# Part of a split of x moved from VectorE to GpSimd, and its loads, clears and copies reordered, in a graph layer on one Trainium2 core

## What is computed

```python
msg = x[src] + edge_attr                                  # [E, 128]
agg = jax.ops.segment_sum(msg, dst, num_segments=N)       # [N, 128]
h = relu(agg @ W1 + b1) @ W2 + b2                         # 128 -> 256 -> 128
# h is normalized over all of its elements, then per feature, then gelu
out = _layernorm(x + (gelu(h) + x))
```

## Time and profile before

| what | value |
|---|---|
| median of 3 runs (lowest, highest) | 750.42 us (748.91, 751.47) |
| the profiled execution's own time | 750.58 us |
| its span in the profile | 748.7 us |
| mean granted TensorE clock | 0.98 |
| PE, DVE, ACT, POOL busy | 92%, 85%, 57%, 16% of the span |
| DMA, mean over the span | 161 GB/s |

### The profile page before, as it was taken

One profiled execution on the slowest core, in us unless ns is written; L12 is line 12 of the kernel. 1 busy time (PEld: TensorE's weight loads), 2 busy tenths in 40 slices (PEclk: granted clock), 3 DMA queues, 4 the chain that ended last, 5 costly groups with the idle time before them and its releaser, 6 DMA issues.

```text
span 748.7 us, 25387 instructions
## 1 busy us (share of the span) xinstructions
PE 692.2 (92%) x9473; PEld 628.3 (84%) x9473; DVE 633.3 (85%) x1067; ACT 424.8 (57%) x962; POOL 116.9 (16%) x91
## 2 busy tenths in 40 slices
PE   4748999999999999999999999999999999999964
PEld 4736888999889988999889988899889998888843
DVE  6698889899899898998989889899898998835576
ACT  6634466546664476645665466645756456514447
POOL 2132110111011110111101110411101111000024
PEclk9997999999999999999999999999999999999986
DMA  7298665356554564536635466255662566400006
GB/s 166 84 338 275 210 202 175 109 178 220 162 177 143 179 215 135 188 130 214 210 103 191 157 220 210 76 193 182 214 189 82 184 214 199 120 16 0 0 1 171
DMA packets 90297, 120.42 MB, mean 161 GB/s; under 512 B 8824, under 2 KB 88190, under 8 KB 90075
## 3 DMA queue, kind: packets, MB, share of 16 engines
q1 hardware_dynamic: 83588, 113.93, 47.0%
q0 software_dynamic: 5776, 5.39, 2.7%
q10 hardware_dynamic: 912, 0.83, 0.6%
HBM read 116.03 MB, written 4.03 MB: 160 GB/s over the span
## 4 chain that ended last, share of the span: by engine, by line
PE 78%; ACT 7%; DMA 5%; DVE 4%; issue 3%; POOL 2%; ACTq 0%; SPq 0%; DVEq 0%; POOLq 0%
PE bank L845 40%; PE bank L787 18%; PE bank L738 10%; ACT counts L617 6%; PE bank L893 3%; PE bank L883 3%; PE bank L752 3%; DMA edges<-in_edge_attr_dram 1%; DMA agg<-pool_m 1%; POOL pool_m L545 1%; PE bank L767 1%; DMA listed<-agg 1%; DMA near<-listed,row_slot 1%; DVE pool_m L1137 1%; DMA begins<-listed,tile_slot 0%
## 5 line engine op out<-in xcount | busy, mean ns | idle before, releaser
L617 ACT CAST counts<-bank 128x490 fp32r<-128x490 f32 x600 | 320.2, 605 | 234.5 <-PE bank L787 231.6
L845 PE MATMUL bank<-counts,x_hi 128*128 128x250 f32 x1225 | 309.0, 292 | 8.9 <-ACT counts L617 8.9
L845 PE MATMUL bank<-counts,x_lo 128*128 128x250 f32 x1225 | 293.5, 279 | 0.0
L845 PEld LDWEIGHTS bank<-counts,x_hi 128*128 128x128 f32 x1225 | 231.0, 189 | 15.2 <-ACT counts L617 14.4
L1137 DVE TENSOR_TENSOR pool_m<-value_row,turned_lo 128x3328 bf16<-128x3328 bf16 (+1 forms) x125 | 229.2, 1834 | 12.8 <-PE bank L787 11.1
L845 PEld LDWEIGHTS bank<-counts,x_lo 128*128 128x128 f32 x1225 | 232.4, 190 | 0.0
L787 PE MATMUL bank<-pool_m 128*128 128x98 bf16 x3125 | 195.3, 210 | 8.2 <-DVE pool_m L1137 4.0
L787 PEld LDWEIGHTS bank<-pool_m 128*128 128x128 bf16 x3125 | 158.4, 99 | 28.1 <-ACT counts L617 7.0
L1137 DVE TENSOR_TENSOR pool_m<-value_row,turned_key 128x2548 bf16<-128x2548 bf16 (+1 forms) x125 | 179.7, 1437 | 0.0
L505 POOL DMA_INDIRECT near<-listed,row_slot x27 | 52.4, 1940 | 495.4 <-DVE tile_slot L992 465.3
L738 PE MATMUL bank<-edges,onehot 128*32 128x128 f32 x3228 | 122.1, 285 | 8.0 <-DMA edges<-in_edge_attr_dram 4.1
(11 more groups left out here) (157 smaller groups left out, 467.0 us busy)
## 6 DMA issues: line engine op xcount, KB each, us to landing
edges<-in_edge_attr_dram SPq DMA_DIRECT2D x134, 768.0 KB, 5.1
out_dram<-pool_m SPq DMA_DIRECT2D x12, 256.0 KB
x_in<-in_x_dram SPq DMA_DIRECT2D x4, 448.0 KB, 5.3
agg<-in_dst_dram SPq DMA_DIRECT2D x1, 768.0 KB
agg<-in_src_dram ACTq DMA_DIRECT2D x1, 768.0 KB
listed<-agg SPq DMA_DIRECT2D x1, 768.0 KB
begins<-listed,tile_slot POOLq DMA_INDIRECT x28, 4.0
near<-listed,row_slot POOLq DMA_INDIRECT x27
```

The costliest lines, as they stand in the source:

```text
L617: nc.scalar.copy(counts[:, :, at:at + NODES], cps[k % RING][:, 0:NODES * NT].rearrange("p (n q) -> p q n", q=NT)).then_inc(banks_free, 1)
L845: last = nc.tensor.matmul(sps[:, 0:CHUNK], part[:, q, :], counts[:, q, at:at + CHUNK], start=(q == 0 and part is x_hi), stop=(q == NT - 1 ...
```

## The change

The change does this:

- `EARLY` is 2, not 4: two pieces of x are loaded ahead of the list, and the remaining 34 tiles (not 20) after the first `gather_near`.
- SP loads H0 as soon as the first `gather_begins` has landed, ahead of the rest of x.
- GpSimd clears columns from 3072 on right behind `gather_begins(0)`; ScalarE clears columns 0 to 3071 by a copy of a zero once the destinations are turned. VectorE waits for both.
- ScalarE makes `x_hi` of pieces 0 and 1 between its two searches, and of the other five when the rest of x is there.
- VectorE makes `x_lo` of pieces 0 and 1 ahead of `stage_row(0)`; GpSimd makes the other five behind `gather_near(1)`, with `gather_begins(2)` after three of them.
- The widening of chunk 1's words moves from VectorE to ScalarE, behind the copies of the first two groups' sums.

```diff
-EARLY = 4
+EARLY = 2
@@ SBUF
+        zero = mv
@@ sync, behind the stores of the list (load and load_pair moved up unchanged)
+            sp.wait_ge(begins_loaded, 16)
+            load(0, 0, 0, 1)
             sp.wait_ge(near_loaded, 16)
...
-            for i in range(2 * LEAD):
+            for i in range(1, 2 * LEAD):
                 load(i // 2, i % 2, i % HALVES, i + 1)
@@ gpsimd
             gather_begins(0)
+            pool.memset(agg[:, GROUP:], 0.0).then_inc(agg_zeroed, 1)
             gather_near(0)
             gather_begins(1)
-            pool.wait_ge(turned, TURNS)
-            pool.memset(agg[:, :], 0.0).then_inc(agg_zeroed, 1)
-            with pool.Fori(1, CHUNKS + 2) as c:
+            gather_near(1)
+            for i in range(EARLY, NT // PIECE):
+                if i == 5:
+                    gather_begins(2)
+                pool.wait_ge(x_high, i + 1)
+                at = slice(i * PIECE, (i + 1) * PIECE)
+                pool.tensor_tensor(x_lo[:, at, :], x_in[:, at, :], x_hi[:, at, :].bitcast(F32), ALU.subtract
+                                   ).then_inc(x_split, 1)
+            with pool.Fori(2, CHUNKS + 2) as c:
                 gather_near(c)
                 gather_begins(c + 1)
@@ scalar
-            search(1)
-            search(2)
...
+            search(1)
             act.wait_ge(x_loaded, 16 * EARLY)
             split_high(0, EARLY)
+            search(2)
+            act.wait_ge(turned, TURNS)
+            nc.scalar.copy(agg[:, 0:GROUP], zero[:, 0:1].to_broadcast([P, GROUP])).then_inc(agg_zeroed, 1)
...
             for g in range(LEAD):
+                if g == GPC:
+                    widen_words(1)
                 copy_sums(g, g % GPC)
@@ vector
             dve.memset(no_edges[:, :], NO_EDGE)
+            dve.memset(zero[:, :], 0.0)
...
+            for i in range(EARLY):
+                split_x(i)
             stage_row(0)
...
             stage_row(1)
-            for i in range(NT // PIECE):
-                split_x(i)
             split_words(1)
-            widen_words(1)
             join_keys(1)
             stage_tile(2)
-            dve.wait_ge(agg_zeroed, 1)
+            dve.wait_ge(agg_zeroed, 2)
```

More of the change, by code:

```diff
@@ L399, in _ @@
             sp.dma_start(listed_full[0:EVEN, :], src_rows[0:EVEN, :]).then_inc(listed_stored, 16)
-            sp.wait_ge(near_loaded, 16)
-            for a, b in ((0, EVEN_LAST), (EVEN_LAST, LAST)):
-                sp.dma_start(x_in[a:b, NT - 1, :], x[(NT - 1) * P + a:(NT - 1) * P + b, :]).then_inc(x_rest_loaded, 16)
-            sp.dma_start(x_in[:, EARLY * PIECE:NT - 1, :], x[EARLY * PIECE * P:(NT - 1) * P, :].rearrange("(t p) d -> p t d", p=P)
-                         ).then_inc(x_rest_loaded, 16)
             def load(g, k, u, free):
@@ L414, in load_pair @@
                          p * (2 * PER_PAIR) + (2 * LEAD + FREED_BY[i] + 1 + HALVES))
-            for i in range(2 * LEAD):
+            sp.wait_ge(begins_loaded, 16)
+            load(0, 0, 0, 1)
+            sp.wait_ge(near_loaded, 16)
+            for a, b in ((0, EVEN_LAST), (EVEN_LAST, LAST)):
+                sp.dma_start(x_in[a:b, NT - 1, :], x[(NT - 1) * P + a:(NT - 1) * P + b, :]).then_inc(x_rest_loaded, 16)
+            sp.dma_start(x_in[:, EARLY * PIECE:NT - 1, :], x[EARLY * PIECE * P:(NT - 1) * P, :].rearrange("(t p) d -> p t d", p=P)
+                         ).then_inc(x_rest_loaded, 16)
+            for i in range(1, 2 * LEAD):
                 load(i // 2, i % 2, i % HALVES, i + 1)
@@ L992, in stage_tile, with split_x @@
                 dve.tensor_copy(tile_slot[0:PAIRS, :], tile_rows[0:PAIRS, bass.ds(c, 1)]).then_inc(tile_staged, 1)
+            def split_x(i):
+                dve.wait_ge(x_high, i + 1)
+                at = bass.ds(i * PIECE, PIECE)
+                dve.tensor_tensor(x_lo[:, at, :], x_in[:, at, :], x_hi[:, at, :].bitcast(F32), ALU.subtract
+                                  ).then_inc(x_split, 1)
             def prep_chain(ins, count):
@@ L1089, in add @@
                 dve.tensor_tensor(at, at, turned_sum[s], ALU.add).then_inc(edges_added, 1)
-            def split_x(i):
-                dve.wait_ge(x_high, i + 1)
-                at = bass.ds(i * PIECE, PIECE)
-                dve.tensor_tensor(x_lo[:, at, :], x_in[:, at, :], x_hi[:, at, :].bitcast(F32), ALU.subtract
-                                  ).then_inc(x_split, 1)
             dve.memset(turned_lo[:, :], -1.0)
```

## The result

The changed kernel takes **757.42 us** (median of 4 runs, 756.98 to 757.98). The kernel before took 749.66 in 4 runs (747.15 to 751.47). The ratio is 1.0106 [1.0074, 1.0138]: slower by 7.8 us. I had forecast 752.4 with a range up to 755.4, so the direction of the sum (+2.0) was right and its size wrong by 5 us. The time lies outside that range.

The account below looks back on a forecast made before the run. TensorE was taken as the bound, its loop untouched, so only the start's relay of hand-overs could shift the end. Terms -0.7, +3.2, +1.7, -1.4, -1.0, +0.2 sum to +2.0: 752.6 profiled, 752.4 median, range 749.2 to 755.4.

Parts of the forecast that it names:

- Two pieces fewer ahead of the list: At the start, fewer bytes of x ahead bring the list and `stage_row(0)` forward by 0.7 us, at most 0.8.
- VectorE's row of chunk 1: `stage_row(1)` ends near 43.6 instead of 47.0, so chunk 1's second gather leaves 3.4 us earlier.
- More x: 14 more tiles (0.92 MB) behind `near(0)` at 282 GB/s add 3.2 us; x lands at 45.2, bounds 44.0 to 46.3.
- Two roundings: ScalarE rounds five pieces instead of three ahead of the first bank copy, on the path: 1.7 us more.
- Waits ahead of H2 and H3: TensorE's waits of 0.60 and 0.82 us for these edge halves go, as they have landed: -1.4 us.
- The widening: On ScalarE behind the second sum's copy, it makes `stage_tile(2)` wait for H3: 57.6 against 55.82, 1.8 us later.
- Idle before H4: TensorE's idle time before H4 no longer ends in VectorE's `add` and shrinks from 3.79 to 2.8 us: -1.0.
- rival B: Faster: shorter idle before H4 keeps the clock at 2.4 GHz, H4 to H7 save 2.6 us; 749.8 to 747.6; chance 0.13.
- Contention: GpSimd's subtractions, 2.4 us each, may hold VectorE's marks of H7 and batch 2; taken as 0.2 us.
- rival A: The lock decides: GpSimd subtractions of 3.3 us or more hold VectorE's batch 2, batch 4 comes late; 754.7, chance 0.22.

Follow-up runs that it names:

- the first experiment: The kernel before with only the clearing in halves, GpSimd's part behind the first gather and ScalarE's behind its roundings: 750.45 us, 1.0004.

## Why the prediction was wrong in size, by its own steps

**Two pieces fewer ahead of the list, -0.7.** Failed. The list's store took 7.11 us, not the 6.61 of the earlier trace rows, and with four pieces ahead of it 7.15 (the first experiment). Two runs with two pieces and little else changed took 5.57 and 7.10, and two of the kernel before 6.61 and 6.07, so no run shows that the bytes of x ahead of it matter. The issue of x came 1.97 us later than in the earlier trace rows. Of that, 0.9 was there when the store began (18.39 against 17.47), behind a first load that arrived 1.5 us later; 0.5 came with the store and 0.8 with the first gather (4.37 us against 3.53), and a little was won back. No step of mine held any of these, and they vary between executions of one kernel.

**VectorE's row of chunk 1, 3.4 us sooner.** Failed, though not a term of the sum. It was to end near 43.6. The first gather of chunk 1 landed only at 47.77, with VectorE idle for 2.18 us, and the second was issued at 49.54, against 47.95 before.

**More x, +3.2.** The first of the two steps that sank the forecast. Issue to landing grew by 12.80 - 7.73 = 5.07 us; alone by 4.1, with edges behind it by 4.1 to 5.9. I divided added bytes by the rate at 40 to 42 and bounded the landing at 46.3 by terms that had nothing to do with the load's own tail.

**Two roundings, +1.7.** Right: 4.30 us for five, and the copy directly behind. **Waits ahead of H2 and H3, -1.4.** Both are gone, and the term was too small: H3 ends 4.41 us after H0 starts, against 6.68 before and my 5.4. H0 to H2 together took 3.20 us, H0 and H1 alone 3.12 before, so this part gave 2.3.

**The widening, `stage_tile(2)` 1.2 us after H3.** Right: 61.23 - 60.04 = 1.19. **Idle before H4, 3.79 to 2.8.** Right: 2.76. Here rival B's condition held for H4 alone, which ran in 0.86 us. Its gain did not come: the hold on `place` followed at once, and H5 and H6 took 2.79 us together, as before.

**Contention, +0.2.** The second step that failed, and rival A named the mechanism. I had the duration about right (2.05 us a piece; I took 2.4, and my estimate from the Trainium skill's figure was 2.0), so rival A's own condition, 3.3 us or more, was not met and yet its mechanism came. I had two things wrong. I let VectorE get in between two GpSimd instructions. The lengths of row say it doesn't: 5.10 us with a gather and two subtractions, 3.08 with a gather and one, and on the words 5.54, 3.52 and 1.53 us, always up to the end of a row of five, four and three. And I priced only marks; what was held is a short operation with one tensor as its source, and it is what TensorE needs for group 1, not for batch 4. I had bounded the effect on batch 2 and behind; it came a batch sooner. From H4's start to H5's the shift grew by 9.01 - 5.41 = 3.6 us.

So the terms as the rows have them are 1.97, 5.07, 1.67, -2.27, -1.03 and 3.60, in sum 9.01, as in the table at H5. Of that, 1.27 are given back up to the first long run (+7.74). The rows of TensorE show where: before, the last twenty bank products and the last half ahead of the first chunk's product ran at the low clock, in 1.81 and 1.49 us from 77.77 on (granted 0.50 at 78 to 80); after, at the full clock, in 1.11 and 0.86 from 86.49 on (1.00 at 86 to 88). These terms are differences of two profiles and add up by construction; the runs that take a part in or out are what shows its price.

The Trainium skill, SBUF — State Buffer, section "SBUF: two separate sides", describes the shared port pair as an exclusive lock for a whole instruction: a VectorE operation in a 2-port performance mode can lose it to any GpSimd operation, one with two SBUF inputs only to a GpSimd operation that reads SBUF. I applied the second half alone. It agrees with VectorE's four subtractions, 6.28 us beside one of GpSimd's and 4.11 without. `place` and the words are of the first kind if they run in such a mode, which no row shows; the memset that held the 21 columns in the earlier trace rows but not the marks fits that. The Trainium skill's wording of one instruction at a time is where the runs differ: a 0.28 us operation was held from inside the gather's issue on and past two subtractions.

**Do the parts add up?** Put in, yes. By medians: H0 ahead with the halves, 748.41 against 749.83, is -1.4; GpSimd's subtractions with the widening on ScalarE, 752.36 against 748.41, is +4.0; two pieces of x moved, 754.98 against 749.83, is +5.2. That gives +7.8, and +7.8 was measured. By the ratios it is -0.22%, +0.53% and +0.66%, in sum 0.97%, against 1.06%. The sum crosses groups of runs on different chips, and the parts were taken on different bases, so the agreement to a few tenths is luck. Taken out of the changed kernel, the same parts give less: four early pieces nothing, the hold 1.5 to 2.3 us by medians (2.0 to 4.0 by ratios), the widening 1.0. What the hold costs in time therefore lies somewhere between 1.5 and 4 us, and how much of the 3.6 us at H5 reaches the end is not settled.

**What stays open.** Why `place` isn't let in between GpSimd's instructions: a held place in the queue, or GpSimd keeping the ports while its next instruction stands ready, would both look like this. The gather's issue alone did not hold `place` in the kernel before nor in nine other profiles, where it began 0.33 us into that issue and took 0.28 us. In six profiles a later `place` began 0.77 us into an issue of 1.45 us, again with no subtraction behind it, and took 0.70 us, up to the end of the issue. With subtractions behind the gather it was held from that same point on, 0.9 us before the first of them starts by its row. An idle gap of known length between two subtractions was not tried. The widening's price (1.2 and 1.0 us, on two bases) is within the intervals. Why the stall of 2.99 us, once gone, gave nothing in the median is open too.

## What to carry to other kernels

Before you price the engine time that a change frees, look at what the work lay beside: 7.12 us of subtractions ended within 0.6 us of a gather's landing, and where three of the seven were taken away the next step came 0.3 us sooner. Two fixed costs of a move are easily missed: bytes moved onto the path can cost more than bytes over rate (here at least 4.1 us, not 3.2), and a long GpSimd instruction that reads can be paid by whatever VectorE operation comes next, here up to the end of GpSimd's unbroken row. So put GpSimd's rows where VectorE's next operation has slack (the five at once did better than the three and two), and look for an empty slot for a transfer, such as the one that H0 moved into.

## What the runs showed of the hardware that was not expected

- A 0.28 us VectorE operation with one source was held for 5.10 and 3.08 us, and a 0.23 us one on the words for 5.54, 3.52 and 1.53 us, each time until the last of GpSimd's consecutive subtractions ended. The first began inside an indirect gather's issue (1.21 us); with no subtraction behind, it took 0.28 us from 0.33 us into such an issue, and 0.70 from 0.77 us into one of 1.45 us, up to its end.
- Four VectorE subtractions, with two sources, took 6.28 us beside one GpSimd subtraction of 2.11 us, and 4.11 without it.
- Loading x in 512-byte rows: 20 tiles 7.6 to 8.2 us, 34 tiles 11.9 us with no edges behind (one run) and 11.8 to 13.6 with edges behind.
- A small indirect gather sent behind one half of edges, at 31.17, took 3.62 us; behind two halves it took 5.74 us.
- The operation that waits for the first load of the program started anywhere between 6.2 and 10.3 us, and at 8.25 and 9.51 in two executions of the same kernel.
